# Rounding in two steps: VectorE takes every first step, ScalarE every second

## The chip, the cores and the metric

The kernel runs on the 8 cores of one Trainium2 chip, one sequence of the batch on each, with no exchange between cores. The metric is the device time of the slowest core, in microseconds (us). The engines are named as in the profile: PE (TensorE, matmul and transpose), PEld (its weight load), DVE (VectorE), ACT (ScalarE), POOL (GpSimd), SP (SyncE).

## What is computed

The input is 8 sequences of 4096 rows with 1024 features, float32. The layer is a feed-forward part, an attention-like part and the same feed-forward part again:

```python
x = x + 0.5 * ffn(layernorm(x), w_gate, w_up, w_down)
x = x + attn(layernorm(x), Wq1, bq1, Wk1, bk1, Wk2, bk2, Wproj, bproj)
x = x + 0.5 * ffn(layernorm(x), w_gate, w_up, w_down)
```

The feed-forward part quantises both weights and activations. Weights go to -1, 0 or 1 times their mean magnitude; activations are scaled row by row to 127 over the row's largest magnitude and rounded to integers:

```python
def _act_quant(x):
    scale = 127.0 / jnp.clip(jnp.max(jnp.abs(x), axis=-1, keepdims=True), 1e-05)
    xq = jnp.clip(jnp.round(x * scale), -128.0, 127.0) / scale
gate = jax.nn.silu(_bitlinear(x, w_gate)); up = _bitlinear(x, w_up)
return _bitlinear(gate * up, w_down)
```

The attention-like part is made of three 1024 x 1024 projections, running sums along the sequence, elementwise products, and an output projection.

## The kernel before

Each core walks its 4096 rows in 8 chunks of 512 rows; a chunk is four groups of 128 rows (tt = 0 to 3). Once at the start a weight stage (`tern_piece`, L301 and L304) rounds the three feed-forward weights and writes them to HBM as bf16. Then for each chunk: feed-forward, attention-like part, feed-forward.

A feed-forward pass has these stages:

- pre (`emit_ffn_pre`): statistics on VectorE, the scaling to integers' range on ScalarE (L517), then eight quads that transpose and round the scaled rows. For the first pass of the next chunk this runs inside the previous pass, between the hidden stage and the down matmuls; for a chunk's second pass it runs right before the gate/up matmuls.
- gate/up (`emit_ffn_rest`, L602 and L607): bf16 matmuls, with ScalarE's Silu (L569) and VectorE's product (L572) and row maximum (L578) behind them.
- hidden: for each tt ScalarE scales the 4096 hidden values of a row (L643, four instructions issued one after the other). Then, tt by tt, `transpose_quads` handles eight quads.
- down (L684): bf16 matmuls with weights loaded by DMAs that ScalarE's queue issues (L665), and the addition to x (L697, L709).

A quad is four 128 x 128 transposes on TensorE (L403 for the first three, L406 for the last) into one of four PSUM buffers, followed by the rounding of the 128 x 512 result. The rounding has two steps. The first adds a constant (`dcol`), converts to int32, which is where the rounding happens, and writes the integer tile `qi32`; the second adds another constant (`nm128_ap`) and writes bf16. The engines share the quads: even ones go to VectorE (first step L420, second step L425, through the half `qiV`), odd ones to ScalarE (L436, L440, through the half `qiS`). Each engine waits before each step for the counter of its own instructions (`cV` or `cS`). TensorE reuses a PSUM buffer when the first step that read it is done. A call of `transpose_quads` without `saved` starts from the counts of that moment, so its first transposes wait for all that VectorE and ScalarE were given before.

`evac="submagic"` selects this rounding; the attention-like part calls the same function with plain copies (L415, L431), which share the engines in the same way. With 16 feed-forward passes there are 16 pre stages of 8 quads and 16 hidden stages of 32.

Of the kernel before, what the change touches and what calls it, by code (L numbers as in the profile page):

```python
# [10 lines left out]
AF = mybir.ActivationFunctionType  # L11
ALU = mybir.AluOpType
# [28 lines left out]
def build_nc(L=4096, T=512):  # L41
# [21 lines left out]
    if DEBUG_ATTN:  # L63
# [41 lines left out]
    qi32 = E(nc.sbuf_tensor("qi32", [128, 1024], I32))  # L105
    qiV = qi32[:, 0:512]
    qiS = qi32[:, 512:1024]
    stats = smal[:, 0:48]
    mv = smal[:, 48:56]
    rstd = smal[:, 56:60]  # L110
# [27 lines left out]
    nm128_ap = smal[:, 187:188]  # L138
    dcol = smal[:, 143:144]
# [16 lines left out]
    cV = Sem(st, nc, "cV")  # L156
    cS = Sem(st, nc, "cS")
    cT = Sem(st, nc, "cT")
    cG = Sem(st, nc, "cG")

    V, S, TE, SY, G = nc.vector, nc.scalar, nc.tensor, nc.sync, nc.gpsimd
# [24 lines left out]
                           scalar1=-2.0, scalar2=-1.0,  # L186
                           op0=ALU.add, op1=ALU.mult))
    cV.wait(V)
    V.tensor_scalar(out=dcol, in0=t1[:, 0:1], scalar1=MAGIC, scalar2=None,
                    op0=ALU.mult)  # L190
    cV.inc(V.tensor_scalar(out=nm128_ap, in0=t1[:, 0:1], scalar1=-MAGIC,
                           scalar2=None, op0=ALU.mult))
    dB.inc(SY.dma_start(out=bsb[:, 0:DC],
                        in_=bq1.ap().rearrange("(j p) -> p j", p=128),
                        allow_slow_non_contiguous=True), 16)
    dB.inc(SY.dma_start(out=bsb[:, DC:2 * DC],
                        in_=bk1.ap().rearrange("(j p) -> p j", p=128),
                        allow_slow_non_contiguous=True), 16)
    dB.inc(SY.dma_start(out=bsb[:, 2 * DC:3 * DC],
                        in_=bk2.ap().rearrange("(j p) -> p j", p=128),  # L200
# [7 lines left out]
                           op0=ALU.mult))  # L208
    dX[0].inc(SY.dma_start(out=xsb[0][:, :, :],
                           in_=x_hbm.ap()[0:T, :]  # L210
# [10 lines left out]
    def tern_dma_in(src_ap, pf):  # L221
        i = tw_state["idx"]
        tw_state["idx"] += 1
        bsel = i % 4
        buf = tpc[bsel][:, 0:pf]
        if tw_state["slotV"][bsel] is not None:
            sem_, n_ = tw_state["slotV"][bsel]
            SY.wait_ge(sem_.h, n_)
        else:
            cV.wait(SY)  # L230
        dTI[bsel].inc(SY.dma_start(out=buf, in_=src_ap), 16)
        return bsel, buf
# [53 lines left out]
    def tern_piece(src_ap, dst_ap, sw_slot, pf, osems, sw_wait=False):  # L286
        bsel, buf = tern_dma_in(src_ap, pf)
        sbf = tst[bsel][:, 0:pf]
        dTI[bsel].wait(V)
        cV.wait(V)  # L290
        cV.inc(V.tensor_scalar(out=buf, in0=buf, scalar1=sw_slot, scalar2=1.4375,
                               op0=ALU.mult, op1=ALU.min))
        cV.wait(V)
        cV.inc(V.tensor_scalar(out=buf, in0=buf, scalar1=-1.4375,
                               scalar2=None, op0=ALU.max))
        prev = tw_state["stgV"][bsel]
        if prev is not None:
            prev[0].wait(V, prev[1])
        for j0 in range(0, pf, 512):
            cV.wait(V)  # L300
            cV.inc(V.tensor_scalar(out=qiV[:, 0:512], in0=buf[:, j0:j0 + 512],  # L301
                                   scalar1=dcol, scalar2=None, op0=ALU.add))
            cV.wait(V)
            cV.inc(V.tensor_scalar(out=sbf[:, j0:j0 + 512], in0=qiV[:, 0:512],  # L304
                                   scalar1=nm128_ap, scalar2=None,
                                   op0=ALU.add))
        tw_state["slotV"][bsel] = (cV, cV.n)
        cV.wait(G)
        osem = osems[bsel]
        osem.inc(G.dma_start(out=dst_ap, in_=sbf), 16)  # L310
        tw_state["stgV"][bsel] = (osem, osem.n)

    def tern_write_gu(w_hbm, scratch, sw_slot, osems):
        for ob in range(8):
            for icg in range(2):
                src = bass.AP(w_hbm, icg * 4 * 128 * INNER + ob * 512,
                              [[INNER, 128], [128 * INNER, 4], [1, 512]])
                dst = bass.AP(scratch, ob * (128 * 8 * 512) + icg * 4 * 512,
                              [[8 * 512, 128], [512, 4], [1, 512]])
                tern_piece(src, dst, sw_slot, 2048, osems,  # L320
                           sw_wait=(ob == 0 and icg == 0))

    def tern_write_d(w_hbm, scratch, sw_slot, osems):
        for icg in range(8):
            for h2 in range(2):
                src = bass.AP(w_hbm, (icg * 4 + h2 * 2) * 128 * D,
                              [[D, 128], [128 * D, 2], [1, D]])
                dst = bass.AP(scratch, icg * (128 * 4 * 1024) + h2 * 2 * 1024,
                              [[4 * 1024, 128], [1024, 2], [1, 1024]])
                tern_piece(src, dst, sw_slot, 2048, osems,  # L330
                           sw_wait=(icg == 0 and h2 == 0))
# [62 lines left out]
    def transpose_quads(quads, evac="copy", eng="alt", saved=None):  # L394
        v0, s0 = saved if saved is not None else (cV.n, cS.n)
        savedV = [v0] * 4
        savedS = [s0] * 4
        for qi, (srcs, dst) in enumerate(quads):
            b = qi % 4
            TE.wait_ge(cV.h, savedV[b])  # L400
            TE.wait_ge(cS.h, savedS[b])
            for j, s_ in enumerate(srcs[:-1]):
                TE.transpose(out=PB[:, b * 1024 + j * 128:  # L403
                                    b * 1024 + (j + 1) * 128],
                             in_=s_, identity=ident[:, :])
            cT.inc(TE.transpose(  # L406
                out=PB[:, b * 1024 + (len(srcs) - 1) * 128:
                       b * 1024 + len(srcs) * 128],
                in_=srcs[-1], identity=ident[:, :]))
            pt = PB[:, b * 1024:b * 1024 + len(srcs) * 128]  # L410
            w_ = len(srcs) * 128
            if eng == "V" or (eng == "alt" and qi % 2 == 0):
                cT.wait(V)
                if evac == "copy":
                    cV.inc(V.tensor_copy(out=dst, in_=pt))  # L415
                    savedV[b] = cV.n
                else:
                    cV.wait(V)
                    assert w_ <= 512
                    cV.inc(V.tensor_scalar(out=qiV[:, 0:w_], in0=pt,  # L420
                                           scalar1=dcol, scalar2=None,
                                           op0=ALU.add))
                    savedV[b] = cV.n
                    cV.wait(V)
                    cV.inc(V.tensor_scalar(out=dst, in0=qiV[:, 0:w_],  # L425
                                           scalar1=nm128_ap, scalar2=None,
                                           op0=ALU.add))
            else:
                cT.wait(S)
                if evac == "copy":  # L430
                    cS.inc(S.copy(out=dst, in_=pt))  # L431
                    savedS[b] = cS.n
                else:
                    cS.wait(S)
                    assert w_ <= 512
                    cS.inc(S.activation(out=qiS[:, 0:w_], in_=pt,  # L436
                                        func=AF.Identity, bias=dcol))
                    savedS[b] = cS.n
                    cS.wait(S)
                    cS.inc(S.add(out=dst, in_=qiS[:, 0:w_],  # L440
                                 add=nm128_ap))

    def xstage(tt):
        hs, ti = tt // 2, tt % 2
# [31 lines left out]
    def emit_ffn_pre(c, xb, first_of_chunk, p, skip01=False):  # L476
# [39 lines left out]
        for tt in range(TT):  # L516
# [3 lines left out]
        cS.inc(sl_)  # L520
        cS.wait(TE)
        transpose_quads(
            [([qstage[:, tt * 1024 + ic * 128:tt * 1024 + (ic + 1) * 128]
               for ic in range(q4 * 4, q4 * 4 + 4)],
# [3 lines left out]
    def emit_ffn_rest(c, xb, p, pre_next=None, attn_next=None):  # L528
# [118 lines left out]
        for tt in range(TT):  # L647
            TE.wait_ge(cS.h, p1_cS[tt])
            transpose_quads(
                [([hbuf[:, tt, ic * 128:(ic + 1) * 128]  # L650
                   for ic in range(q * 4, q * 4 + 4)],
                  hq[:, tt, q * 4:q * 4 + 4, :]) for q in range(8)],
                evac="submagic", saved=hq_saved)
            hq_saved = None
# [460 lines left out]
    for c in range(NCH):  # L1115
        xb = xsb[c % 2]
        if c + 1 < NCH:
            if c >= 1:
                dO.wait(SY, 16 * c)
            dX[(c + 1) % 2].inc(SY.dma_start(  # L1120
                out=xsb[(c + 1) % 2][:, :, :],
                in_=x_hbm.ap()[(c + 1) * T:(c + 2) * T, :]
# [6 lines left out]
        if c + 1 < NCH:  # L1129
# [6 lines left out]
            out=y_hbm.ap()[c * T:(c + 1) * T, :].rearrange("(a p) d -> p a d",  # L1136
                                                           p=128),
            in_=xb[:, :, :]), 16)
# [29 lines left out]
```

## Time and profile before

| what | value |
|---|---|
| median of 2 runs | 6813.15 us (6764.25 and 6862.05) |
| the profiled execution, its own time | 6789.98 us |
| its span, slowest core (core 2) | 6788.9 us |
| spans of the 8 cores | 6704.3 to 6788.9 us |
| PE busy | 4037.0 us, 59% |
| DVE busy | 2602.9 us, 38% |
| ACT busy | 1579.8 us, 23% |
| POOL busy | 489.5 us, 7% |
| DMA | 699.97 MB, 103 GB/s on average |

No engine is busy all the time: the stages follow each other, and each has its own limit. The page lists busy time by engine and by line, and a chain that leads back from the last instruction through what each step waited for. A time that is on that chain is not hidden behind other work.

### The profile page before, as it was taken

How to read it: one execution, taken by the hardware profiler on the slowest of the kernel's cores; microseconds unless marked ns; L12 is line 12 of the kernel's file. 1: busy time of each engine (PE TensorE's matmuls, PEld its weight loads, DVE VectorE, ACT ScalarE, POOL GpSimd, SP SyncE). 2: the span in 40 equal slices, each digit the busy share in tenths (PEclk: the TensorE clock that was granted, in tenths of full speed). 3: DMA queues.
4: the chain of work that ended last, by engine and by line, in shares of the span. 5: the costliest groups of instructions: out<-in, count | busy, mean ns of one | idle time of the engine just before them, and what ended most of it. 6: DMA issues, size and time to landing. Idle time of an engine off the chain costs nothing.

```text
span 6788.9 us, 56589 instructions; the slowest of 8 cores (6704.3 to 6788.9 us)
## 1 busy us (share of the span) xinstructions
PE 4037.0 (59%) x18745; PEld 2128.6 (31%) x19026; DVE 2602.9 (38%) x4295; ACT 1579.8 (23%) x2080; POOL 489.5 (7%) x505
## 2 busy tenths in 40 slices
PE   0006646686377754686475763686466763777457
PEld 0002333334233331333233341333333341333323
DVE  4554244332532325423442316422443325422442
ACT  2110221322231321302212311302213221312212
POOL 0000020000200011000200012000200002000200
PEclk6557768878697876898687886898788886888778
DMA  6884243144233252242432262242431352242522
GB/s 207 243 258 147 73 81 99 56 124 99 50 100 116 82 107 63 66 153 75 79 106 79 101 121 53 69 150 83 84 99 56 124 111 57 81 123 88 93 81 88
DMA packets 229226, 699.97 MB, mean 103 GB/s; under 512 B 22096, under 2 KB 22096, under 8 KB 224848
## 3 DMA queue, kind: packets, MB, share of 16 engines
q10 hardware_dynamic: 110592, 402.70, 18.5%
q0 software_dynamic: 76576, 159.41, 12.9%
q1 hardware_dynamic: 41776, 134.24, 6.4%
q8 instruction: 161, 2.64, 0.2%
q14 instruction: 121, 0.99, 0.1%
HBM read 788.55 MB, written 41.94 MB: 122 GB/s over the span
## 4 chain that ended last, share of the span: by engine, by line
PE 42%; DVE 23%; ACT 13%; DMA 13%; issue 7%; POOL 1%; DVEq 1%; ACTq 0%; SPq 0%; POOLq 0%
PE PB L607 12%; PE PB L602 11%; PE PB L684 9%; DMA sarena<-sc_d 7%; PE PB L754 5%; PE PB L403 4%; ACT qi L436 2%; DVE pool L572 2%; ACT poolb L440 2%; ACT pool L643 2%; DMA sarena<-sc_u 2%; DVE qi L301 1%; DVE poolb L304 1%; ACT pool L770 1%; DVE smal L578 1%
## 5 line engine op out<-in xcount | busy, mean ns | idle before, releaser
L607 PE MATMUL PB<-sarena,poolb 128*128 128x512 bf16 x4096 | 1615.4, 394 | 210.3 <-DVE smal L535 121.6
L602 PE MATMUL PB<-sarena,poolb 128*128 128x512 bf16 x3927 | 1548.5, 394 | 155.1 <-DVE smal L578 83.2
L684 PE MATMUL PB<-sarena,poolb 128*128 128x512 bf16 x4000 | 957.8, 396 | 213.8 <-DMA sarena<-sc_d 208.8
L403 PE MATMUL PB<-ident,pool 128*128 128x128 f32 x2144 | 489.3, 364 | 962.6 <-ACT pool L517 367.1
L572 DVE SCALAR_TENSOR_TENSOR pool<-PB,smal,pool 128x512 f32<-128x512 f32 x512 | 381.9, 746 | 1364.6 <-ACT pool L569 1364.6
L602 PEld LDWEIGHTS PB<-sarena,poolb 128*128 128x128 bf16 x4096 | 412.1, 101 | 940.0 <-issue 566.5
L403 PEld LDWEIGHTS PB<-ident,pool 128*128 128x128 f32 x2144 | 373.3, 194 | 1001.9 <-issue 1000.2
L569 ACT ACTIVATE pool<-PB,smal 128x512 f32<-128x512 f32 x512 | 326.3, 684 | 1466.8 <-PE PB L607 1436.2
L684 PEld LDWEIGHTS PB<-sarena,poolb 128*128 128x128 bf16 x4096 | 401.6, 101 | 765.8 <-issue 384.8
L607 PEld LDWEIGHTS PB<-sarena,poolb 128*128 128x128 bf16 x4096 | 412.0, 101 | 495.7 <-issue 122.0
L754 PE MATMUL PB<-poolb 128*128 128x256 bf16 x3072 | 410.1, 302 | 159.7 <-ACT pool L770 125.4
L697 DVE SCALAR_TENSOR_TENSOR xsb<-PB,smal,xsb 128x512 f32<-128x512 f32 x64 | 43.6, 744 | 1146.7 <-PE PB L684 1146.7
L420 DVE TENSOR_SCALAR qi<-PB,smal 128x512 int32<-128x512 f32 x320 | 240.2, 751 | 432.4 <-PE PB L406 417.9
L754 PEld LDWEIGHTS PB<-poolb 128*128 128x128 bf16 x3072 | 326.1, 107 | 243.8 <-issue 175.6
L578 DVE TENSOR_REDUCE smal<-pool 128x1 f32<-128x512 f32 x512 | 351.2, 686 | 55.0 <-DVE pool L572 2.7
L734 POOL DMA_DIRECT2D poolb<-wk1t x64 | 45.8, 720 | 4364.4 <-PE PB L684 4277.1
L1030 PE MATMUL PB<-poolb 128*128 128x512 bf16 x496 | 200.7, 580 | 264.4 <-DMA poolb<-wpt 138.7
L436 ACT ACTIVATE qi<-PB,smal 128x512 int32<-128x512 f32 x320 | 220.1, 688 | 155.4 <-PE PB L406 134.7
L643 ACT ACTIVATE pool<-pool,smal 128x4096 f32<-128x4096 f32 x64 | 232.1, 3697 | 61.3 <-DVE smal L627 57.5
L1017 PE MATMUL PB<-bprow,onesrb 1*128 1x512 bf16 x64 | 29.8, 615 | 352.8 <-DVE poolb L941 352.8
L569 ACT ACT_TABLE_LOAD x16 | 20.5, 1283 | 937.2 <-PE PB L607 937.2
L440 ACT ACTIVATE poolb<-qi,smal 128x512 bf16<-128x512 int32 x320 | 231.0, 722 | 30.3 <-ACT qi L436 0.7
(139 smaller groups left out, 3201.7 us busy)
## 6 DMA issues: line engine op xcount, KB each, us to landing
sarena<-sc_g ACTq DMA_DIRECT2D x256, 512.0 KB, 4.2
sarena<-sc_u ACTq DMA_DIRECT2D x256, 512.0 KB, 5.2
sarena<-sc_d ACTq DMA_DIRECT2D x256, 512.0 KB, 3.8
pool<-wgt SPq DMA_DIRECT2D x32, 1024.0 KB, 9.9
pool<-wut SPq DMA_DIRECT2D x32, 1024.0 KB, 8.7
pool<-wdt SPq DMA_DIRECT2D x32, 1024.0 KB, 9.9
poolb<-wk1t POOLq DMA_DIRECT2D x64, 512.0 KB, 8.5
poolb<-wq1t POOLq DMA_DIRECT2D x64, 512.0 KB, 7.4
```

Of the source, the lines that this page charges most:

```text
L403: TE.transpose(out=PB[:, b * 1024 + j * 128: b * 1024 + (j + 1) * 128], in_=s_, identity=ident[:, :])
L420: cV.inc(V.tensor_scalar(out=qiV[:, 0:w_], in0=pt, scalar1=dcol, scalar2=None, op0=ALU.add))
L436: cS.inc(S.activation(out=qiS[:, 0:w_], in_=pt, func=AF.Identity, bias=dcol))
L440: cS.inc(S.add(out=dst, in_=qiS[:, 0:w_], add=nm128_ap))
L569: cS.inc(S.activation(out=sl, in_=pb[ttg * 4 + (tt % 2)][:, :], func=AF.Silu, scale=cg[:, tt:tt + 1]))
L572: cV.inc(V.scalar_tensor_tensor(out=hbuf[:, tt, ob_ * 512:(ob_ + 1) * 512], in0=pb[ttg * 4 + 2 + (tt % 2)][:, :], scalar=cu[:, tt:tt + 1], ...
L578: cV.inc(V.reduce_max(out=hpart[:, tt * 8 + ob_:tt * 8 + ob_ + 1], in_=hbuf[:, tt, ob_ * 512:(ob_ + 1) * 512], axis=AXX, apply_absolute_va ...
L602: TE.matmul(out=pb[ttg * 4 + (tt % 2)][:, :], lhsT=aq[:, tt, ic, :], rhs=gsl[:, bsel * 2048 + ic4 * 512: bsel * 2048 + (ic4 + 1) * 512], s ...
L607: tl_ = TE.matmul(out=pb[ttg * 4 + 2 + (tt % 2)][:, :], lhsT=aq[:, tt, ic, :], rhs=usl[:, bsel * 2048 + ic4 * 512: bsel * 2048 + (ic4 + 1) ...
L643: cS.inc(S.activation(out=hbuf[:, tt, :], in_=hbuf[:, tt, :], func=AF.Identity, scale=s2v[:, tt:tt + 1]))
L684: tl_ = TE.matmul(out=pb[tt * 2 + obk][:, :], lhsT=hq[:, tt, ic, :], rhs=dsl[:, bsel * 2048 + ic2 * 1024 + obk * 512: bsel * 2048 + ic2 * ...
L754: tl_ = TE.matmul(out=pb[et][:, 0:HT], lhsT=aw_tile(dc, et), rhs=xn2T[:, dc, rhs_off + th * HT: rhs_off + th * HT + HT], start=(dc == 0), ...
```

## The change

In `transpose_quads` the rounding is taken out of the sharing of quads between the engines. VectorE does the first step of every quad, ScalarE the second step of every quad. The two halves of the integer tile become two slots that both engines use in turn, even quads `qiV` and odd quads `qiS`. Before a first step VectorE waits for the second step that last read the slot (`slot_op2`); before a second step ScalarE waits for VectorE's counter. The waits of each engine for its own counter around the rounding are gone. TensorE's reuse of a PSUM buffer now waits on VectorE alone. The weight stage, which writes `qiV` too, gets a wait for the slot. The copies of the attention-like part keep their order.

```diff
+    slot_op2 = [0, 0]
@@ tern_piece
+        V.wait_ge(cS.h, slot_op2[0])
         for j0 in range(0, pf, 512):
@@ transpose_quads
-            if eng == "V" or (eng == "alt" and qi % 2 == 0):
+            if evac != "copy":
+                assert w_ <= 512
+                slot = (qiV if qi % 2 == 0 else qiS)[:, 0:w_]
                 cT.wait(V)
-                if evac == "copy":
-                    cV.inc(V.tensor_copy(out=dst, in_=pt))
-                    savedV[b] = cV.n
-                else:
-                    cV.wait(V)
-                    assert w_ <= 512
-                    cV.inc(V.tensor_scalar(out=qiV[:, 0:w_], in0=pt,
-                                           scalar1=dcol, scalar2=None,
-                                           op0=ALU.add))
-                    savedV[b] = cV.n
-                    cV.wait(V)
-                    cV.inc(V.tensor_scalar(out=dst, in0=qiV[:, 0:w_],
-                                           scalar1=nm128_ap, scalar2=None,
-                                           op0=ALU.add))
+                V.wait_ge(cS.h, slot_op2[qi % 2])
+                cV.inc(V.tensor_scalar(out=slot, in0=pt,
+                                       scalar1=dcol, scalar2=None,
+                                       op0=ALU.add))
+                savedV[b] = cV.n
+                cV.wait(S)
+                cS.inc(S.add(out=dst, in_=slot, add=nm128_ap))
+                slot_op2[qi % 2] = cS.n
+            elif eng == "V" or (eng == "alt" and qi % 2 == 0):
+                cT.wait(V)
+                cV.inc(V.tensor_copy(out=dst, in_=pt))
+                savedV[b] = cV.n
             else:
                 cT.wait(S)
-                if evac == "copy":
-                    cS.inc(S.copy(out=dst, in_=pt))
-                    savedS[b] = cS.n
-                else:
-                    cS.wait(S)
-                    assert w_ <= 512
-                    cS.inc(S.activation(out=qiS[:, 0:w_], in_=pt,
-                                        func=AF.Identity, bias=dcol))
-                    savedS[b] = cS.n
-                    cS.wait(S)
-                    cS.inc(S.add(out=dst, in_=qiS[:, 0:w_],
-                                 add=nm128_ap))
+                cS.inc(S.copy(out=dst, in_=pt))
+                savedS[b] = cS.n
```

## Rows read from the trace of the kernel before

**Rows 1.** Page, its head and the chain that ended last, by line

```profile
span 6788.9 us, 56589 instructions; the slowest of 8 cores (6704.3 to 6788.9 us)
...
PE PB L607 12%; PE PB L602 11%; PE PB L684 9%; DMA sarena<-sc_d 7%; PE PB L754 5%; PE PB L403 4%; ACT qi L436 2%; DVE pool L572 2%; ACT poolb L440 2%; ACT pool L643 2%; DMA sarena<-sc_u 2%; DVE qi L301 1%; DVE poolb L304 1%; ACT pool L770 1
```

**Rows 2.** Groups by line: engine, tile, shape, count; busy us, mean ns; idle before

```profile
L420 DVE TENSOR_SCALAR qi<-PB,smal 128x512 int32<-128x512 f32 x320 | 240.2, 751 | 432.4 <-PE PB L406 417.9 <-DVE poolb L425 0.2
...
L440 ACT ACTIVATE poolb<-qi,smal 128x512 bf16<-128x512 int32 x320 | 231.0, 722 | 30.3 <-ACT qi L436 0.7
L436 ACT ACTIVATE qi<-PB,smal 128x512 int32<-128x512 f32 x320 | 220.1, 688 | 155.4 <-PE PB L406 134.7 <-ACT pool L643 0.4 <-ACT poolb L440 0.4
...
L425 DVE TENSOR_SCALAR poolb<-qi,smal 128x512 bf16<-128x512 int32 x320 | 155.6, 486 | 35.0 <-DVE qi L420 0.9
```

**Rows 3.** Timeline, last hidden stage, tt = 0: start us, length us, engine, line

```profile
6663.76 14.51 ACT L643 ACTIVATE pool<-pool,smal 128x4096 f32<-128x4096 f32 x4 [3.77 <-DVE smal L627]
...
6683.92 0.72 ACT L440 ACTIVATE poolb<-qi,smal 128x512 bf16<-128x512 int32 x1
```

**Rows 4.** Timeline, the next block of eight quads (tt = 1)

```profile
6684.79 0.87 PE L403 MATMUL PB<-ident,pool 128*128 128x128 f32 x3 [2.81 <-ACT poolb L440]
...
6686.05 0.75 DVE L420 TENSOR_SCALAR qi<-PB,smal 128x512 int32<-128x512 f32 x1 [3.40 <-PE PB L406]
...
6686.88 0.69 ACT L436 ACTIVATE qi<-PB,smal 128x512 int32<-128x512 f32 x1 [2.24 <-PE PB L406]
...
6692.44 0.72 ACT L440 ACTIVATE poolb<-qi,smal 128x512 bf16<-128x512 int32 x1
```

**Rows 5.** Timeline, the block after it (tt = 2)

```profile
6693.31 0.52 PE L403 MATMUL PB<-ident,pool 128*128 128x128 f32 x3 [3.37 <-ACT poolb L440]
...
6694.11 0.75 DVE L420 TENSOR_SCALAR qi<-PB,smal 128x512 int32<-128x512 f32 x1 [2.10 <-PE PB L406]
...
6694.52 0.69 ACT L436 ACTIVATE qi<-PB,smal 128x512 int32<-128x512 f32 x1 [1.36 <-PE PB L406]
...
6700.09 0.72 ACT L440 ACTIVATE poolb<-qi,smal 128x512 bf16<-128x512 int32 x1
```

**Rows 6.** Windows: us, busy (count) PE, PEld, DVE, ACT, POOL, PEclk, DMA, GB/s

```profile
728.54:753.63 25.09, 16.80 (x96) 16.06 (x96) 14.84 (x24) 16.91 (x24) 0.00 (x0) 0.69 0.00 1
...
6684.64:6709.09 24.45, 15.85 (x96) 15.15 (x96) 14.85 (x24) 16.91 (x25) 0.00 (x0) 0.80 0.00 1
sum 391.56, PE 249.72 PEld 236.24 DVE 243.88 ACT 270.63 POOL 0.00; mean PE 15.61 PEld 14.77 DVE 15.24 ACT 16.91 POOL 0.00
```

**Rows 7.** Waits: engine, line, released by, us in total, times, longest

```profile
PE PB L403 <- ACT pool L517: 367.1, 16, 38.9
...
PE PB L403 <- ACT poolb L440: 139.2, 48, 3.4
```

**Rows 8.** Timeline of ScalarE, then of VectorE, in a gate/up stage

```profile
5846.55 0.69 ACT L569 ACTIVATE pool<-PB,smal 128x512 f32<-128x512 f32 x1 [2.19 <-PE PB L607]
...
5844.74 0.69 DVE L578 TENSOR_REDUCE smal<-pool 128x1 f32<-128x512 f32 x1
5845.34 0.74 DVE L572 SCALAR_TENSOR_TENSOR pool<-PB,smal,pool 128x512 f32<-128x512 f32 x1
...
5847.34 0.75 DVE L572 SCALAR_TENSOR_TENSOR pool<-PB,smal,pool 128x512 f32<-128x512 f32 x1 [0.47 <-ACT pool L569]
```

**Rows 9.** Timeline, what follows the last block when no next chunk is prepared

```profile
6708.44 53.56 ACTq L665 DMA_DIRECT2D sarena<-sc_d  x14
...
6713.18 9.44 PE L684 MATMUL PB<-sarena,poolb 128*128 128x512 bf16 x31 [6.88 <-DMA sarena<-sc_d]
```

**Rows 10.** Timeline, what follows it when the next chunk is prepared

```profile
5925.02 0.49 DVE L425 TENSOR_SCALAR poolb<-qi,smal 128x512 bf16<-128x512 int32 x1
5925.56 0.72 ACT L440 ACTIVATE poolb<-qi,smal 128x512 bf16<-128x512 int32 x1
5925.61 0.69 DVE L348 BATCH_NORM_STATS2 smal<-xsb 128x6 f32<-128x512 f32 x1
```


## The prediction

> **What bounds the kernel now.** I read the page first, for the chain that ended last, then the groups by line, then the timeline of the hidden-quantising stage, where most of the changed code runs. The chain by line [rows 1] is to show two things: TensorE's large matmuls (L607, L602, L684) carry most of it, and the changed ScalarE lines L436 and L440 are on it with 2% each. So the rounding is not hidden, but it is a small part: 2% + 2% of 6788.9 us is some 270 us. The groups [rows 2] give its four instructions: VectorE's first step L420 751 ns and second step L425 486 ns, ScalarE's L436 688 ns and L440 722 ns, 320 of each. These 640 quads fall into 80 blocks of eight: 16 hidden stages with four blocks (tt = 0 to 3), and 16 pre stages with one.
>
> The timeline shows how a block goes. In the block tt = 1 [rows 4] TensorE starts at 6684.79, VectorE takes the first quad at 6686.05 (1.26 us later), ScalarE the second at 6686.88 (0.83 us behind it), and the last L440 ends at 6692.44 + 0.72 = 6693.16. Only then does TensorE start the next block, at 6693.31 [rows 5], 0.15 us later, because each block's first wait names everything counted so far. The wait table confirms it: 48 times TensorE waited for L440, 139.2 us in all [rows 7]. From one block's end to the next it is 6693.16 - 6684.64 = 8.52 us for tt = 1 (6684.64 being 6683.92 + 0.72 [rows 3]). For tt = 2 it is 7.65 us [rows 5]: there TensorE's transposes run fast at first (three in 0.52 us instead of 0.87, the 2.4 GHz level instead of 1.2), VectorE starts after 0.80 us and ScalarE 0.41 us behind it. Over all 48 such blocks the mean is 391.56 / 48 = 8.16 us [rows 6]; the granted clock is 0.69 in the first of these stretches and 0.80 in the last. Within a block ScalarE sets the pace: its quads follow each other every (6692.44 - 6686.88 + 0.72 + 0.10) / 4 = 1.60 us, that is 0.688 + 0.722 and two gaps of about 0.09. Two engines at 1.60 and less per quad give 0.80 us per quad.
>
> **What the change does to a block.** VectorE now does the first step of all eight quads, ScalarE the second. The busy time hardly moves: ScalarE 2 x 722 = 1444 instead of 688 + 722 = 1410 ns for two quads, VectorE 2 x 751 = 1502 instead of 1237. What changes is the order. Gone is the wait of each engine for its own last instruction. The gate/up block shows what that is worth [rows 8]: L572 starts at 5845.34, 0.60 us after the start of the 0.69 us long L578, so an instruction that need not wait overlaps the one before by 0.09. VectorE could thus take a quad every 0.75 - 0.09 = 0.66 us (I take the same overlap for ScalarE: 0.72 - 0.09 = 0.63).
>
> New are two crossings between engines, tied by only two integer slots. A slot is written by VectorE (0.75), crosses, is read by ScalarE (0.72), crosses back, and only then takes the quad after next. A crossing costs 0.10 us: L569 ends at 5846.55 + 0.69 = 5847.24 and L572, which waited for it, starts at 5847.34 [rows 8]. I take 0.10 for both directions. One turn of a slot is 0.75 + 0.10 + 0.72 + 0.10 = 1.67 us for two quads, 0.84 per quad: slower than either engine alone, and slower than the 0.80 of now. This turn, I expect, sets the pace.
>
> A block is then: 0.15 to start, the wait for the first quad, the lag of the second behind it, three turns for slot 1 (quads 1, 3, 5, 7) = 5.02, and the last quad's 0.75 + 0.10 + 0.72 = 1.57 us.
> With a slow start: 0.15 + 1.26 + 0.83 + 5.02 + 1.57 = 8.83 against 8.52, +0.31.
> With a fast start: 0.15 + 0.80 + 0.66 + 5.02 + 1.57 = 8.20 against 7.65, +0.55.
> The mean of 8.16 lies (8.16 - 7.65) / (8.52 - 7.65) = 0.59 of the way to the slow kind, so the mean cost is 0.59 x 0.31 + 0.41 x 0.55 = 0.41 us, and 48 x 0.41 = 19.6 us. The 16 pre stages find TensorE idle for 367.1 / 16 = 23 us before them [rows 7], so they start slow: 16 x 0.31 = 5.0 us.
>
> The block tt = 0 is different. ScalarE is busy with the four scalings L643 until 6663.76 + 14.51 = 6678.27 [rows 3]. VectorE's new wait for a slot stops it after two quads; behind it on its queue stand only more first steps, which the same ScalarE work will need anyway. The two waiting second steps, overlapping L643 by the same 0.09, take ScalarE from 6678.18 to 6678.90 and from 6678.81 to 6679.53, VectorE starts quad 2 at 6679.00 and quad 3 at 6679.66, two turns later (3.35) quad 7 at 6683.01, and it is done at 6684.58 against 6684.64 now. That is -0.06 x 16 = -1 us. TensorE has six quads ready by then instead of five, which saves nothing: quad 6 is ready about 6679.75 + 1.26 = 6681.0, before VectorE wants it at 6682.35.
>
> **What comes behind.** Where the down matmuls follow, their first load is issued at 6708.44, right behind the start of the last L440 at that stage's end, and TensorE starts 4.7 us later on its landing [rows 9]: the load moves with L440, so nothing hides the added time. Where the next chunk is prepared first, its statistics wait on VectorE's own queue: L425 ends at 5925.02 + 0.49 = 5925.51 and L348 starts at 5925.61 [rows 10]. ScalarE's last L440 ended 5925.56 + 0.72 = 5926.28, 0.77 us behind VectorE's; in the new order VectorE's last step ends 0.10 + 0.72 = 0.82 us before ScalarE's, so this delay is the same too. The wait put into the weight stage is for a second step done long before, and costs nothing; if that cover were gone it would be one slot's 0.82 us, once.
>
> Sum: 19.6 + 5.0 - 1 = +24 us, or +0.35%.
>
> **Rivals.**
> A. The engines set the pace, not the slots (a crossing overlaps like two instructions of one engine). The quads then come every 0.66 us: a fast block is 0.15 + 0.80 + 7 x 0.66 + 1.57 = 7.14, -0.51; a slow one is held by the transposes, about 0.85 us apart (the lag of 0.83 [rows 4]), for its first half, some 0.15 + 1.26 + 3 x 0.83 + 4 x 0.66 + 1.57 = 8.11, -0.41. About -0.45 x 64 = -29 us. For it: the overlap of rows 8. Against it: the 0.10 after L569 in the same rows.
> B. VectorE is held to 0.75 + 0.10 = 0.85 us per quad, even without the wait for itself. Quad 7 starts 7 x 0.85 = 5.95 us behind quad 0, against 5.68 and 5.85 above: +0.10 to +0.27 per block, another 64 x 0.18 = 12 us, +36 in all. Against it stand the 0.60 us of rows 8.
> The Trainium skill, page "VectorE: DVE Perf Modes", section "The DRAIN you can't avoid", says so in effect: leaving out semaphores between VectorE instructions gains nothing, since the pipeline empties between them anyway. By that rule B holds; rows 8 speak against it.
> C. Slower by over 2%: the crossings cost far more, because each engine now checks two counters before each step and both work on the same integer tile. 2% is 136 us; 112 us beyond my sum over 80 blocks x 3 turns is 0.47 us a turn, so it decides from a crossing of 0.10 + 0.23 = 0.33 us. The nearest rows, 0.10 for a crossing [rows 8] and 0.15 for one to TensorE [rows 5], are far below.
> D. It changes nothing that can be measured in the path, because what waits behind a block waits for something else. Against it: the 48 waits of rows 7 and the load of rows 9. It would give +0.
> E. Faster by over 2% needs 136 / 80 = 1.7 us a block, more than A gives with both engines at their best. Only another share of TensorE's fast level could do that, and nothing in the rows points there.
>
> **How the numbers follow.** The forecast has 0.62, A 0.13, B 0.10, C 0.06, D 0.05, E 0.04. The sum is made against the profiled execution's 6789.98 us and gives 6814; that run lies 23 us under the median 6813.15 of the two others (6764.25 and 6862.05), against which it would be 6837. I say 6820. The unknown is less the change than that spread. Low: A from a quick run, 6764 - 29 = 6735, little of which is needed for 8 in 10: 6745. High: B from the slower run, 6862 + 36 = 6898: 6900. About 2% is what a measurement of this kernel can tell from no change; faster by more than that 0.04 (E), slower by more 0.06 (C), within 0.90.
>
> **What would show it.** Right, if in the new timeline the first steps of quads q and q + 2 start 1.67 us apart and each second step starts 0.10 us after its first; if the 16 windows over tt = 1 to 3 sum to 391.56 + 20 = 411 us; if the block tt = 0 ends 6.3 us after L643; if VectorE's idle before the first step is put down to ScalarE. A shows first steps 0.66 us apart in a fast block and a sum near 370. B shows first steps 0.85 apart with no wait for ScalarE between them. C shows turns above 2.1 us. I am wrong if a crossing is not 0.10, if the first steps on VectorE no longer take 0.75, or if TensorE spends another share of the stage at 1.2 GHz.

## The result and the profile after

The changed kernel takes 6816.35 us (median of 43 runs) against 6791.61 us for the kernel before (42 runs of the same comparison). The ratio is 1.0043 with a 95% interval of 1.0023 to 1.0063: slower by 29 us, between 16 and 43. The medians take in all executions, the ratio leaves out those (about a third with the changed kernel) in which the cores of one die run slower. The profiled execution of the changed kernel has a span of 6774.9 us on core 7, less than the 6788.9 us on core 2 before: two single executions differ by more than the change does, so the comparison below is made inside the blocks and not between spans.

The chain by line, from the page of the changed kernel, answers to [rows 1]. The first step (now L419) is on it with 4%, the second step (L424) with 2%.

```profile
PE PB L594 11%; PE PB L599 10%; PE PB L676 8%; DMA sarena<-sc_d 8%; PE PB L746 4%; DVE qi L419 4%; PE PB L405 4%; DVE pool L564 3%; ACT pool L635 3%; ACT poolb L424 2%; DMA sarena<-sc_u 2%; DMA poolb<-wq1t 2%; DVE poolb L306 1%; DVE qi L303 1%; DVE smal L570 1%
```

The groups by line of the changed kernel, against [rows 2]: count, busy us, mean ns, and what ended the idle time before them. The durations are the same, 749 and 721 ns, and VectorE's idle time before the first steps is too, 431.3 us against 432.4. What ended it has changed: 154.1 us of it are now put down to ScalarE's second steps. Most of that, 132.5 us, is the stop of 8.3 us in each of the 16 blocks tt = 0; within the other blocks it comes in pieces of 0.26.

```profile
L419 DVE TENSOR_SCALAR qi<-PB,smal 128x512 int32<-128x512 f32 x640 | 469.7, 749 | 431.3 <-PE PB L408 246.7 <-ACT poolb L424 154.1
L424 ACT ACTIVATE poolb<-qi,smal 128x512 bf16<-128x512 int32 x640 | 451.8, 721 | 214.7 <-DVE qi L419 179.1
```

The last hidden stage on VectorE, from the timeline: start, length and count of quads. The first three rows are quads 2 to 7 of tt = 0, then follow tt = 1 (slow) and tt = 2 (fast).

```profile
6660.62 1.41 DVE L419 TENSOR_SCALAR qi<-PB,smal 128x512 int32<-128x512 f32 x2 [8.29 <-ACT poolb L424]
6662.29 1.41 DVE L419 TENSOR_SCALAR qi<-PB,smal 128x512 int32<-128x512 f32 x2 [0.26 <-ACT poolb L424]
6663.97 1.41 DVE L419 TENSOR_SCALAR qi<-PB,smal 128x512 int32<-128x512 f32 x2 [0.26 <-ACT poolb L424]
6667.61 6.63 DVE L419 TENSOR_SCALAR qi<-PB,smal 128x512 int32<-128x512 f32 x8 [2.23 <-PE PB L408]
6676.00 1.41 DVE L419 TENSOR_SCALAR qi<-PB,smal 128x512 int32<-128x512 f32 x2 [1.77 <-PE PB L408]
6677.67 1.41 DVE L419 TENSOR_SCALAR qi<-PB,smal 128x512 int32<-128x512 f32 x2 [0.26 <-ACT poolb L424]
```

In the fast block a pair of first steps takes 1.41 us, 0.66 + 0.75: the second of the pair overlaps the first. Then VectorE stands for 0.26 us until ScalarE has emptied the slot, and the next pair starts 6677.67 - 6676.00 = 1.67 us after the last. That is the turn of a slot. ScalarE's rows in the same block:

```profile
6676.85 1.38 ACT L424 ACTIVATE poolb<-qi,smal 128x512 bf16<-128x512 int32 x2 [1.80 <-DVE qi L419]
...
6681.87 1.38 ACT L424 ACTIVATE poolb<-qi,smal 128x512 bf16<-128x512 int32 x2 [0.29 <-DVE qi L419]
```

The first step of quad 0 ends at 6676.00 + 0.75 = 6676.75, its second starts at 6676.85: a crossing of 0.10. The block ends at 6681.87 + 1.38 = 6683.25.

The windows over the blocks tt = 1 to 3 of the 16 hidden stages, the last and the sum, answer to [rows 6]; the first number is the length:

```profile
6666.19:6692.29 26.10, 16.36 (x96) 15.36 (x96) 17.38 (x24) 16.89 (x25) 0.00 (x0) 0.80 0.00 1
sum 415.63, PE 257.48 PEld 239.63 DVE 287.76 ACT 273.37 POOL 0.00; mean PE 16.09 PEld 14.98 DVE 17.98 ACT 17.09 POOL 0.00
```

415.63 against 391.56 us is +24.1 us. (The expectations below take this sum as 414, which is 1.6 us short.) The block tt = 0 ends 6.31 us behind the scalings on average, against 6.41: -1.6 us over 16 stages. The 16 pre stages, read in the same way from the end of the scaling (L517 before, L509 after) to the last second step, take 9.27 instead of 8.91 us: +5.9. Together +28 us, within the 16 to 43 that was measured. Over all 8 cores of the two profiled executions the three parts together take 26.9 us more on average, of which 22.6 are the 48 blocks.

One thing in these blocks is not the order of the steps. A block starts fast when TensorE's transposes run at 2.4 GHz as it begins, which puts VectorE's first step about 0.95 us behind the block before it; with 1.2 GHz it is about 1.41. Before, 27 of the 48 blocks started fast (23 to 27 on the 8 cores), after the change only 15 (15 to 19). Twelve blocks are fast throughout in both kernels. Why more of the others begin at 1.2 GHz was not tested.

### The profile page after: what moved, and what is told of

It is laid out like the page before. It is cut to its first block, busy times and chain, and to the rows that moved or that the text cites. A ratio compares the mean times of both kernels' runs of the same rounds, so it can differ in the third digit from the quotient of the medians.

```text
span 6774.9 us, 56918 instructions; the slowest of 8 cores (6715.3 to 6774.9 us)
## 1 busy us (share of the span) xinstructions
PE 3997.1 (59%) x19026; PEld 2105.8 (31%) x19026; DVE 2676.6 (40%) x4295; ACT 1578.0 (23%) x2080; POOL 488.2 (7%) x505
## 4 chain that ended last, share of the span: by engine, by line
PE 39%; DVE 26%; DMA 14%; ACT 11%; issue 7%; DVEq 1%; POOL 1%; ACTq 0%; SPq 0%; POOLq 0%
PE PB L594 11%; PE PB L599 10%; PE PB L676 8%; DMA sarena<-sc_d 8%; PE PB L746 4%; DVE qi L419 4%; PE PB L405 4%; DVE pool L564 3%; ACT pool L635 3%; ACT poolb L424 2%; DMA sarena<-sc_u 2%; DMA poolb<-wq1t 2%; DVE poolb L306 1%; DVE qi L303 1%; DVE smal L570 1%
## 5 line engine op out<-in xcount | busy, mean ns | idle before, releaser
L405 PE MATMUL PB<-ident,pool 128*128 128x128 f32 x2144 | 494.2, 366 | 979.3 <-ACT pool L509 373.1
L594 PEld LDWEIGHTS PB<-sarena,poolb 128*128 128x128 bf16 x4096 | 406.8, 99 | 940.3 <-issue 502.0
L419 DVE TENSOR_SCALAR qi<-PB,smal 128x512 int32<-128x512 f32 x640 | 469.7, 749 | 431.3 <-PE PB L408 246.7
L676 PEld LDWEIGHTS PB<-sarena,poolb 128*128 128x128 bf16 x4096 | 395.7, 100 | 761.3 <-issue 349.4
L599 PEld LDWEIGHTS PB<-sarena,poolb 128*128 128x128 bf16 x4096 | 406.6, 99 | 477.2 <-issue 37.1
L424 ACT ACTIVATE poolb<-qi,smal 128x512 bf16<-128x512 int32 x640 | 451.8, 721 | 214.7 <-DVE qi L419 179.1
L408 PE MATMUL PB<-ident,pool 128*128 128x128 f32 x672 | 238.5, 355 | 0.0
```

Source lines behind the costliest of these rows:

```text
L405: TE.transpose(out=PB[:, b * 1024 + j * 128: b * 1024 + (j + 1) * 128], in_=s_, identity=ident[:, :])
L408: cT.inc(TE.transpose(out=PB[:, b * 1024 + (len(srcs) - 1) * 128: b * 1024 + len(srcs) * 128], in_=srcs[-1], identity=ident[:, :]))
L419: cV.inc(V.tensor_scalar(out=slot, in0=pt, scalar1=dcol, scalar2=None, op0=ALU.add))
L424: cS.inc(S.add(out=dst, in_=slot, add=nm128_ap))
L594: TE.matmul(out=pb[ttg * 4 + (tt % 2)][:, :], lhsT=aq[:, tt, ic, :], rhs=gsl[:, bsel * 2048 + ic4 * 512: bsel * 2048 + (ic4 + 1) * 512], s ...
L599: tl_ = TE.matmul(out=pb[ttg * 4 + 2 + (tt % 2)][:, :], lhsT=aq[:, tt, ic, :], rhs=usl[:, bsel * 2048 + ic4 * 512: bsel * 2048 + (ic4 + 1) ...
```

## The experiments

The times are ratios of each kernel to the kernel before, measured beside it on the same chip (one chip for e1 to e4, a second for e5 to e8, a third for e9 and e10). Of e4 and e10 there is one execution each. The columns of blocks come from each profile in the way just shown.

| run | ratio (95% interval) | 48 blocks tt = 1 to 3, us | tt = 0, mean us |
|---|---|---|---|
| before | 1 | 391.6 | 6.41 |
| changed | 1.0043 (1.0023 to 1.0063) | 415.6 | 6.31 |
| e1, four slots | 0.9941 (0.9909 to 0.9973) | 377.2 | 4.90 |
| e2, roles swapped | 0.9907 (0.9877 to 0.9936) | 357.3 | 5.90 |
| e3, own waits behind | 1.0132 (1.0103 to 1.0161) | 444.8 | 7.16 |
| e4, one slot | one run, 7270.52 us | 706.9 | 12.35 |
| e5, own waits ahead | 1.018 (1.0092 to 1.0268) | 476.9 | 7.61 |
| e6, changed and chained | 0.9943 (0.9901 to 0.9985) | 323.1 | 6.31 |
| e7, before and chained | 0.9848 (0.9757 to 0.994) | 306.9 | 6.41 |
| e8, swapped, chained, four slots | 0.9685 (0.9605 to 0.9764) | 228.8 | 5.77 |
| e9, swapped, chained, two slots | 0.9785 (0.9735 to 0.9836) | 266.6 | 5.89 |
| e10, slot wait first | one run, 6839.45 us | 422.1 | 6.52 |

**e1: four slots instead of two.** The theory was that the turn of a slot sets the pace; the rival, that VectorE or the crossings do so whatever the number of slots.

```diff
-                slot = (qiV if qi % 2 == 0 else qiS)[:, 0:w_]
+                slot = qslots[qi % 4][:, 0:w_]
...
-                V.wait_ge(cS.h, slot_op2[qi % 2])
+                V.wait_ge(cS.h, slot_op2[qi % 4])
```

`qslots` holds `qiV`, `qiS` and two more slots, in the tile that the Silu uses in the gate/up stage.

> The changed kernel with four integer slots instead of two (the idle silu tile lends two). Theory, the turn of a slot sets the pace: with four slots a turn of 1.67 us serves four quads, so the engines or the transposes set it. Fast blocks 7.1 us, slow ones 8.1, the 48 blocks tt = 1 to 3 sum to about 370 us (two slots: 414), tt = 0 ends about 5.1 us behind the scalings (two slots: 6.3); -29 and -22 us against the kernel before, ratio 0.9925. Rival, the pace comes from the crossings or from VectorE itself and not from the number of slots: blocks as with two slots, sum 414, ratio 1.004.

The timeline of VectorE in the last block of e1: the pairs alternate between the two integer tiles, and no row has a wait for ScalarE.

```profile
6644.37 1.41 DVE L421 TENSOR_SCALAR qi<-PB,smal 128x512 int32<-128x512 f32 x2 [1.76 <-PE PB L410]
6645.70 1.40 DVE L421 TENSOR_SCALAR pool<-PB,smal 128x512 int32<-128x512 f32 x2
6647.01 1.40 DVE L421 TENSOR_SCALAR qi<-PB,smal 128x512 int32<-128x512 f32 x2
6648.33 1.40 DVE L421 TENSOR_SCALAR pool<-PB,smal 128x512 int32<-128x512 f32 x2
```

The pairs are 1.32 us apart, 0.66 per quad, and the fast block takes 7.13 us (expected 7.1). The blocks that start slow take 8.26 us on average, more than the 8.1 expected, so the sum is 377 and not 370; the block tt = 0 was a little better, 4.90. The same split of the work, with two slots more, is faster than the kernel before. The loss of the change is in the number of slots.

**e2: the roles swapped.** ScalarE does every first step (688 ns), VectorE every second (486 ns), with two slots. TensorE's counter is waited for by ScalarE, and TensorE waits for ScalarE before it reuses a PSUM buffer. The weight stage no longer needs its wait for the slot, which VectorE now frees itself.

```diff
-                cT.wait(V)
-                V.wait_ge(cS.h, slot_op2[qi % 2])
-                cV.inc(V.tensor_scalar(out=slot, in0=pt, scalar1=dcol, ...))
-                cV.wait(S)
-                cS.inc(S.add(out=dst, in_=slot, add=nm128_ap))
...
+                cT.wait(S)
+                S.wait_ge(cV.h, slot_op2[qi % 2])
+                cS.inc(S.activation(out=slot, in_=pt, func=AF.Identity, bias=dcol))
...
+                cS.wait(V)
+                cV.inc(V.tensor_scalar(out=dst, in0=slot, scalar1=nm128_ap, ...))
```

> The changed kernel with the roles swapped: ScalarE does every first step (688 ns), VectorE every second (486 ns), still two slots. Theory, a turn is the sum of both steps and two crossings: 0.69 + 0.10 + 0.49 + 0.10 = 1.38 us instead of 1.67; fast block 0.15 + 0.80 + 0.60 + 3 x 1.38 + 1.28 = 6.97, slow one held by the transposes 7.7 to 8.1; sum of the 48 blocks about 361 us, tt = 0 5.9 to 6.0; some -49 us against before, ratio 0.993. Rival, only the fact of alternating engines costs: ratio 1.004 as in the changed kernel.

VectorE's second steps in a fast block of e2, from the timeline:

```profile
6606.91 1.06 DVE L423 TENSOR_SCALAR poolb<-qi,smal 128x512 bf16<-128x512 int32 x2 [1.83 <-ACT qi L419]
6608.29 1.07 DVE L423 TENSOR_SCALAR poolb<-qi,smal 128x512 bf16<-128x512 int32 x2 [0.31 <-ACT qi L419]
```

The turn is 1.38 us, as expected to the hundredth; fast blocks take 7.01 to 7.03 (6.97), the sum is 357.3 (361) and tt = 0 takes 5.90. With two slots and the same crossings the time follows the sum of the two durations in a turn.

**e3 and e5: the own waits put back.** Both add each engine's wait for its own counter before both steps. In e3 it stands behind the other waits, in e5 ahead of them.

```diff
                 cT.wait(V)
                 V.wait_ge(cS.h, slot_op2[qi % 2])
+                cV.wait(V)          # e3; in e5 ahead of cT.wait(V)
                 cV.inc(V.tensor_scalar(out=slot, ...))
                 cV.wait(S)
+                cS.wait(S)          # e3; in e5 ahead of cV.wait(S)
                 cS.inc(S.add(out=dst, ...))
```

> The changed kernel with each engine's wait for its own last instruction put back before both steps, slots and crossings unchanged. Theory (the turn sets the pace, and leaving out the own wait gains the overlap of 0.09 and the gap of 0.10): VectorE's first steps 0.85 us apart instead of 0.66 within a pair, fast blocks 8.20 + 0.27, slow ones + 0.10, about +12 us over the changed kernel, ratio 1.006. Rival, the pipeline empties between two instructions anyway, so the own wait costs nothing: first steps as far apart as in the changed kernel, ratio 1.004.

> As the kernel with the own waits put back, but each own wait stands before the waits for the other engines instead of behind them. Theory: the wait that releases last is cheap (0.10) when it is the last before its instruction and dearer (0.15 to 0.18, as in the kernel with the own wait last) when another wait stands behind it. So here crossings are back at 0.10 and VectorE's own pace of 0.85 rules: a pair every 1.70 us instead of 1.80, fast blocks 8.4 to 8.5, slow ones 8.9, tt = 0 about 6.4, ratio to before 1.006. Rival: the third wait costs wherever it stands: pairs every 1.80, blocks 8.9 to 9.35, tt = 0 7.06, ratio 1.013.

VectorE and ScalarE in a fast block of e3, then VectorE and ScalarE in a block of e5 (timelines):

```profile
6769.45 1.61 DVE L420 TENSOR_SCALAR qi<-PB,smal 128x512 int32<-128x512 f32 x2 [0.19 <-PE PB L408]
6771.25 1.61 DVE L420 TENSOR_SCALAR qi<-PB,smal 128x512 int32<-128x512 f32 x2 [0.19 <-PE PB L408]
...
6773.04 1.61 DVE L420 TENSOR_SCALAR qi<-PB,smal 128x512 int32<-128x512 f32 x2 [0.18 <-ACT poolb L426]
...
6770.35 1.58 ACT L426 ACTIVATE poolb<-qi,smal 128x512 bf16<-128x512 int32 x2 [0.22 <-DVE qi L420]
```

```profile
6793.37 0.75 DVE L420 TENSOR_SCALAR qi<-PB,smal 128x512 int32<-128x512 f32 x1 [0.24 <-DVE qi L420]
6794.37 0.75 DVE L420 TENSOR_SCALAR qi<-PB,smal 128x512 int32<-128x512 f32 x1 [0.24 <-DVE qi L420]
...
6794.22 0.72 ACT L426 ACTIVATE poolb<-qi,smal 128x512 bf16<-128x512 int32 x1 [0.27 <-DVE qi L420]
```

e3 confirms that the own wait costs VectorE its overlap: a pair now lasts 1.61 us and not 1.41. But it cost more than I had expected, 1.0132 and not 1.006, because the crossings grew too. The first step ends at 6769.45 + 0.75 = 6770.20 and its second starts at 6770.35, 0.15 later; that one ends at 6771.07 and VectorE goes on at 6771.25, 0.18 later. (Two of the rows name TensorE, whose transposes ended close to that second step; the third, at 6773.04, names ScalarE with the same 0.18.) The pair takes 1.80 us.

For e5 I expected the crossings back at 0.10 and the ratio at 1.006. The crossing to ScalarE did come back: 6793.37 + 0.75 = 6794.12 to 6794.22 is 0.10. But the whole was slower still, 1.018. The rows show why: VectorE's gap is 0.24 us after each of its own steps, so a quad takes 0.995 us. I had overlooked that on VectorE the own wait was now the one that releases, and that two other waits stood behind it. Over the changed kernel, e3 and e5 the gap after a release was 0.10 with no wait behind the releasing one, 0.15 (ScalarE) and 0.18 (VectorE) with one, 0.24 with two. The trace has each wait as an instruction of its own: in a later block of e5 VectorE's three waits start at 6806.10, 6806.17 and 6806.24 and the step at 6806.31, so each wait takes 0.07 us of VectorE's queue even when its counter has long been reached. My reason for e5 was right and my arithmetic for it wrong. The rival (the same cost wherever the wait stands) is out by the rows, where two quads take 1.99 us in e5 and 1.80 in e3; its ratio of 1.013 lies within e5's interval, while the 1.006 of my theory does not. e10 tests the reason by itself.

**e10: only the order of two waits.**

```diff
-                cT.wait(V)
                 V.wait_ge(cS.h, slot_op2[qi % 2])
+                cT.wait(V)
```

> The changed kernel with VectorE's two waits in the other order: first the slot (ScalarE's counter), then TensorE's. Theory from the runs with the own waits: a wait that releases costs 0.10 if it is the last before its instruction and 0.05 to 0.08 more for each wait behind it. The slot wait is the one that releases in most turns, so a pair of quads takes 1.74 instead of 1.67 us, a fast block 8.4 instead of 8.20. Rival: the order of waits does not matter: pairs stay at 1.67, fast blocks at 8.20.

VectorE in a fast block of e10, from the timeline:

```profile
6741.51 1.41 DVE L419 TENSOR_SCALAR qi<-PB,smal 128x512 int32<-128x512 f32 x2 [1.70 <-PE PB L408]
6743.25 1.41 DVE L419 TENSOR_SCALAR qi<-PB,smal 128x512 int32<-128x512 f32 x2 [0.33 <-ACT poolb L424]
```

The pairs are 1.74 us apart, as expected, and the idle time is 0.33 instead of 0.26. The fast blocks take 8.34 (expected 8.4, the changed kernel 8.20), the sum is 422 us instead of 416. The order of two waits is worth 0.07 us a turn. The block grows by 0.14 and not by three times that, because at its start TensorE's wait, now the last, is the one that releases: VectorE begins 0.07 us sooner (idle 1.70 instead of 1.77).

**e4: one slot.**

```diff
-                slot = (qiV if qi % 2 == 0 else qiS)[:, 0:w_]
+                slot = qiV[:, 0:w_]
-                V.wait_ge(cS.h, slot_op2[qi % 2])
+                V.wait_ge(cS.h, slot_op2[0])
```

> The changed kernel with one integer slot for all quads. Theory: each quad takes a whole turn of 1.67 us; blocks 0.15 + 0.80 (or 1.26) + 7 x 1.67 + 1.57 = 14.2 to 14.7 us, tt = 0 about 12.5, sum of the 48 blocks about 695 us; +500 us, ratio 1.073. Rival, transposes or PSUM buffers set the pace and the slot wait is hidden: blocks under 9 us, within 1% of the changed kernel.

The timeline of VectorE in e4:

```profile
6644.88 0.75 DVE L419 TENSOR_SCALAR qi<-PB,smal 128x512 int32<-128x512 f32 x1 [0.92 <-ACT poolb L424]
6646.55 0.75 DVE L419 TENSOR_SCALAR qi<-PB,smal 128x512 int32<-128x512 f32 x1 [0.93 <-ACT poolb L424]
```

Each quad takes 1.67 us. Blocks take 14.68 to 15.07 us, nearly all of them 14.69, and tt = 0 12.3. All 48 start slow, so the 14.2 expected of a fast start never came and the sum is 707 and not 695. At 7270.52 us the one run is 1.075 times the 6765.4 us of the kernel before on that chip; 1.073 was expected. One, two and four slots give 1.67, 0.84 and 0.66 us per quad: the turn over the number of slots, until VectorE itself is the limit.

**e6 and e7: the blocks chained.** The calls for tt = 0 to 3 pass on which PSUM buffers are free, instead of starting from everything counted so far. `transpose_quads` takes the two lists of counts as `carry` and updates them in place. The diff shows the hidden stage:

```diff
+        carry = ([hq_saved[0]] * 4, [hq_saved[1]] * 4)
         for tt in range(TT):
             TE.wait_ge(cS.h, p1_cS[tt])
             transpose_quads(
...
-                evac="submagic", saved=hq_saved)
-            hq_saved = None
+                evac="submagic", carry=carry)
```

> The changed kernel, but in the hidden stage the four calls of the transposing function pass on which PSUM buffers are free, so a block no longer waits for all that went before. Theory: the 24 quads of tt = 1 to 3 run on at the turn of a slot, 0.84 us each, 20.1 us a stage instead of 25.9 (sum 322 instead of 414); -92 us against the changed kernel, ratio to before 0.991. Rival, the transposes set the pace once they run on (0.85 us each at 1.2 GHz): 20.5 us, nearly the same time, but VectorE's first steps then wait for TensorE and not for ScalarE.

> The kernel before with the same chaining, engines sharing the quads as before. Theory: ScalarE's 1.60 us for every second quad sets the pace, 24 quads in 19.2 us instead of 24.5 (sum 307 instead of 392); -85 us, ratio 0.9875, and the changed order keeps its disadvantage of 0.04 us a quad. Rival: with the waits between blocks gone both orders are held by TensorE and come out equal.

The sums of the windows over tt = 1 to 3, for e6 and then for e7:

```profile
sum 323.12, PE 207.14 PEld 139.32 DVE 267.05 ACT 265.30 POOL 0.00; mean PE 12.95 PEld 8.71 DVE 16.69 ACT 16.58 POOL 0.00
```

```profile
sum 306.91, PE 175.94 PEld 137.85 DVE 234.01 ACT 270.72 POOL 0.00; mean PE 11.00 PEld 8.62 DVE 14.63 ACT 16.92 POOL 0.00
```

322 and 307 were expected. Without the fill and drain of each block the pace of the two orders stands alone: 6.70 us for eight quads (four turns of 1.67) in the changed order, 6.38 (four times 1.60) in the old one. The changed order loses 16.2 us over 384 quads, 0.042 a quad, of which the two paces give (6.70 - 6.38) / 8 = 0.040; the rest is in the few blocks that take longer than these. The rival, that TensorE holds both, is out: the orders do not come out equal, and in e6 VectorE's pairs still start a turn apart:

```profile
6635.97 1.41 DVE L420 TENSOR_SCALAR qi<-PB,smal 128x512 int32<-128x512 f32 x2 [0.27 <-PE PB L409]
6637.64 1.41 DVE L420 TENSOR_SCALAR qi<-PB,smal 128x512 int32<-128x512 f32 x2 [0.27 <-PE PB L409]
```

(These rows name TensorE, but the transposes of the second pair's first quad had ended at 6635.92, 1.7 us before.) The chaining is worth 85 us in the blocks of the old order and 93 in those of the changed one, more than anything that the change touches.

**e9 and e8: roles swapped and blocks chained, with two and with four slots.** Both put the diffs of e2 and e6 together; e8 has the four slots of e1 too.

> ScalarE every first step, VectorE every second, hidden blocks chained, but two slots instead of four. Theory: a turn of 0.69 + 0.10 + 0.49 + 0.10 = 1.38 us serves two quads, 0.69 us a quad: 24 quads in 16.5 us, sum 264 (four slots: 229), some 35 to 45 us slower than with four slots, ratio to before about 0.974. Rival: ScalarE itself sets the pace in both, so two slots do as well as four: sum 229, ratio 0.9685.

> All that helped together: ScalarE every first step, VectorE every second, four slots, hidden blocks chained. Theory: no turn binds, ScalarE's 0.60 us a quad does: 24 quads in 14.4 us when the transposes run at 2.4 GHz, up to 20.4 while they run at 1.2; sum 240 to 290 instead of 392, tt = 0 5.4 us instead of 6.4; ratio 0.972 to 0.981. Rival: the swap of roles gained through something other than the turn, so four slots add nothing to it: first steps stay 0.69 us apart on average, ratio above 0.983.

The sums for e9 and then for e8:

```profile
sum 266.65, PE 203.09 PEld 143.71 DVE 186.78 ACT 240.31 POOL 0.00; mean PE 12.69 PEld 8.98 DVE 11.67 ACT 15.02 POOL 0.00
```

```profile
sum 228.77, PE 194.81 PEld 149.60 DVE 186.70 ACT 217.64 POOL 0.00; mean PE 12.18 PEld 9.35 DVE 11.67 ACT 13.60 POOL 0.00
```

With two slots eight quads take 5.50 us, 0.69 each (expected 0.69; sum 264). With four they take 4.63, 0.58 each, 38 us less in all. So the turn binds the swapped order too, and its gain in e2 came from the shorter turn. e8 is the fastest kernel of this study, 3.15% below the kernel before; its blocks were faster than the 240 to 290 us expected, since the transposes, run on without a pause, were seldom the limit: 35 of the 48 blocks take 4.62 to 4.63 us, the other 13 take 4.83 to 5.61 (in e8's whole span ScalarE waited 43 us for transposes). The block tt = 0 took 5.77, not the 5.4 expected.

The pace of 0.58 in e8 is ScalarE's. The timeline of VectorE and ScalarE in its last blocks:

```profile
6514.03 1.06 DVE L426 TENSOR_SCALAR poolb<-qi,smal 128x512 bf16<-128x512 int32 x2
6515.19 1.06 DVE L426 TENSOR_SCALAR poolb<-pool,smal 128x512 bf16<-128x512 int32 x2
...
6514.27 1.39 ACT L422 ACTIVATE pool<-PB,smal 128x512 int32<-128x512 f32 x2
6515.41 1.40 ACT L422 ACTIVATE qi<-PB,smal 128x512 int32<-128x512 f32 x2
```

VectorE's second steps last 0.49 us and start 0.58 apart, but they are not free to start earlier: each waits for its first step, and each of the 384 in these blocks starts 0.10 to 0.11 us after that first step ends (6514.27 + 1.39 = 6515.66, and the second step of that quad starts 0.58 behind 6515.19, at 6515.77). No backlog builds up in front of VectorE, so it follows ScalarE. ScalarE in turn is held by neither of the others: at these rows the transposes of a quad had ended 0.7 us and its slot had come free 0.9 us before the first step began. I had named ScalarE at 0.60; its first steps start 0.57 apart. What holds ScalarE to that, and why its rows grow from 0.67 to 0.85 us each as the stage goes on, is open.

## Why the prediction was right

**The path.** The rounding was held to be on the path and not hidden, with 48 waits of TensorE for the last second step [rows 7]. After the change there are 49 such waits, 145.8 us in all, and the +28 us found in the blocks are what the clock of the whole kernel shows, 29 us. The prediction's "most of it" for the three large matmuls was too strong: 12% + 11% + 9% is 32% of the chain, its largest part. Rival D, no effect, is out by the interval and by e6 and e7, where a gain inside the blocks came out as a gain of the kernel.

**The turn.** 1.67 us were worked out from a crossing of 0.10 that was read off a quite different pair of instructions [rows 8]; 1.67 was measured. The fast block was put at 8.20 us, and it is 8.20. The slow one was put at 8.83; the row tt = 1 above gives 8.86, and 8.84 to 8.92 is the usual size. There the turn is not alone in setting the pace: with TensorE at 1.2 GHz the transposes of a quad take 0.85 us, as much as half a turn, and VectorE's first steps follow them for the first quads before the slots take over. The two cannot be told apart in a slow block; the fast blocks, e1 and e4 tell them apart. The prediction gave the whole slow block to the turn although its rival A had the 0.85.

The 48 blocks cost 24.1 us and not 19.6. The 12 blocks that are fast throughout rose by the 0.55 forecast; the other 36 rose by 0.48 on average, and not by 0.31. The rows show 12 more of them starting at 1.2 GHz. The prediction had listed another share of the stage at 1.2 GHz as a sign of being wrong, and this sign did come, for a quarter of the blocks. Split by start, fast starts average 8.23 us against 7.89 and slow ones 8.85 against 8.50: 0.35 us a block or 17 us in all, and the 12 further slow starts make the remaining 7. A pre stage cost 0.37 and not 0.31.

**The block tt = 0.** VectorE stopped after two quads, for 8.29 us, and the block ended 0.10 us earlier than before; 0.06 was worked out.

**VectorE's idle time.** It was to be put down to ScalarE. That holds for tt = 0 and for part of the turns only: 246.7 us before first steps are still put down to TensorE, 154.1 to ScalarE.

**The overlap.** VectorE's first steps follow each other by 0.66 us within a pair. So rival B (0.85 a quad even without the own wait) is out by these rows; its +36 us is inside the measured interval of 16 to 43, so the time alone would not have excluded it. With it falls, for these instructions, what was drawn from the Trainium skill's page "VectorE: DVE Perf Modes", section "The DRAIN you can't avoid": e3 and e5 show that a wait between two VectorE instructions did cost time here, 0.20 and 0.34 us between their starts. The section also says that a next instruction that is not held starts earlier, and with that the 0.66 us agree.

**Rival A**, the engines set the pace, did not happen with two slots, but its arithmetic for a fast block was sound: its 7.14 us is the 7.13 of e1. Its slow block of 8.11 was too cheap, e1's slow starts average 8.26, and where it put the sum near 370 e1 has 377.

**Rival C**, dear crossings, needed 0.33 us for a crossing. 0.10 was found. What it pointed to, an engine that checks several counters before a step, is real but smaller: 0.05 to 0.08 us for each wait behind the releasing one. The change has two waits on VectorE and happens to have the one that releases within a turn, the slot's, last, where it costs nothing more.

**The time.** +24 us were worked out, +29 measured; 6820 us forecast, 6816.35 measured. The mechanism carried the sign and most of the size, 17 + 6 - 2 us of the 28 in the rows; the rest is the slow starts, which no term held. That the time agrees within 4 us is luck: single executions of the kernel before spread over 6745 to 6952 us.

## What to carry to other kernels

When two engines hand a tile to each other, work out the turn of a buffer (write, cross, read, cross back) and divide it by the number of buffers; if that is above the busier engine's own pace, the split costs time though no engine has more to do, and another buffer or the shorter of two ways to share the steps gives it back. Look at what stands around the loop before tuning inside it: here the drain between blocks was worth 85 to 93 us and the change of order within them cost 24. Put the wait that is usually last to be met last in front of its instruction.

## What the runs showed of the hardware

- Two VectorE instructions of 0.75 us with no wait for each other started 0.66 us apart; with an own wait standing last, 0.86; with the own wait first and two more behind it, 0.995.
- The gap after a release depended on the waits behind the releasing one: 0.10 us with none, 0.15 to 0.18 with one, 0.24 with two; in e5's trace VectorE's waits follow one another 0.07 us apart. e10 changed only the order and moved a turn by the 0.07 expected.
- After the change fewer blocks began with TensorE at 2.4 GHz, 15 of 48 instead of 27, on every core in the same direction. The cause is open.
- A crossing between VectorE and ScalarE took 0.10 us in both directions when the releasing wait was the last.
- In e8 ScalarE's first steps started 0.57 us apart, overlapping, with records of 0.67 to 0.85 us, and each second step on VectorE started 0.10 to 0.11 behind the end of its first. What sets ScalarE's pace is open.
